# Feed-forward rows turned by VectorE in 32 by 32 blocks and moved through DRAM, in place of six TensorE transposes a tile

## The reference

```python
def _L0_attn_ref(X, W_Q, W_K, W_V):
    D = _get_D(L)                                   # 0.9 ** |n - m|
    Q = _xpos(X @ W_Q); K = _xpos(X @ W_K, downscale=True); V = X @ W_V
    p_attn = softmax(einsum('bqd,bkd->bqk', Q, K), axis=-1) * D[None, :, :]
    return einsum('bqk,bkv->bqv', p_attn, V)

def _L0_ffn_ref(x, w_gate, w_up, w_down):           # fp4_linear quantises both operands
    gate = fp4_linear(x, w_gate)                    # 256 -> 704
    y = fp4_linear(x, w_up)
    h = silu(gate) * y
    return fp4_linear(h, w_down)                    # 704 -> 256

x = x + _L0_attn_ref(_layernorm(x), W_Q, W_K, W_V)
x = x + _L0_ffn_ref(_layernorm(x), w_gate, w_up, w_down)
```

## Time and profile before

| what | value |
|---|---|
| time, three runs | 2548.14, 2549.42, 2549.66 us (median 2549.42) |
| span of the profiled execution | 2546.6 us |
| PE busy, share, instructions | 2518.4 us, 99%, 16160 |
| DVE | 2140.9 us, 84%, 4759 |
| ACT | 1489.8 us, 59%, 2966 |
| POOL | 1816.8 us, 71%, 1929 |
| DMA | 203.27 MB, 24.1% of the 16 engines on the main queue |
| HBM | 103.42 MB read, 77.59 MB written |

### The profile page before, as it was taken

One profiled execution on the slowest core, in us unless ns is written; L12 is line 12 of the kernel. 1 busy time (PEld: TensorE's weight loads), 2 busy tenths in 40 slices (PEclk: granted clock), 3 DMA queues, 4 the chain that ended last, 5 costly groups with the idle time before them and its releaser, 6 DMA issues.

```text
span 2546.6 us, 51904 instructions
## 1 busy us (share of the span) xinstructions
PE 2518.4 (99%) x16160; PEld 2290.0 (90%) x16160; DVE 2140.9 (84%) x4759; ACT 1489.8 (59%) x2966; POOL 1816.8 (71%) x1929
## 2 busy tenths in 40 slices
PE   8999999999999999999999999999999999999997
PEld 7888879999999999999999999999999999999996
DVE  8999878888878888888888888888888888888886
ACT  5766565656555655566565656565556655555654
POOL 6999956667767676667766776677666776677665
PEclk9999999999999999999999999999999999999999
DMA  8878511122111311131112111131113111211110
GB/s 285 302 271 299 186 50 30 34 86 66 38 40 45 107 37 42 34 106 42 42 34 91 62 38 40 45 107 39 42 34 106 41 42 34 95 58 38 40 38 22
DMA packets 163473, 203.27 MB, mean 80 GB/s; under 512 B 15184, under 2 KB 116752, under 8 KB 163216
## 3 DMA queue, kind: packets, MB, share of 16 engines
q1 hardware_dynamic: 163216, 200.01, 24.1%
HBM read 103.42 MB, written 77.59 MB: 71 GB/s over the span
## 4 chain that ended last, share of the span: by engine, by line
PE 85%; POOL 0%; DVE 0%; issue 0%; ACT 0%; POOLq 0%
PE score L516 27%; PE acc L655 19%; PE ring L516 19%; PE acc L516 9%; PE ring L622 6%; PE ring L675 3%; PE acc L697 1%; PE ring L613 1%; DVE hT L1226 0%; POOL probs L998 0%; ACT probs L823 0%; ACT hT L793 0%; POOL h_buf L1019 0%; POOL xv L1004 0%; POOL h_buf L1013 0%
## 5 line engine op out<-in xcount | busy, mean ns | idle before, releaser
L516 PE MATMUL score<-keys,q_st 128*128 128x512 f32 x3072 | 733.7, 394 | 3.0 <-ACT probs L823 2.6
L516 PEld LDWEIGHTS score<-keys,q_st 128*128 128x128 f32 x3072 | 567.0, 188 | 117.8 <-issue 3.0
L998 POOL TENSOR_TENSOR probs<-probs,decay 128x512 f32<-128x512 f32 (+3 forms) x416 | 450.7, 1097 | 197.5 <-ACT probs L823 197.5
L655 PE MATMUL acc<-vals,pT 128*128 128x256 f32 x3984 | 554.6, 286 | 0.8 <-DVE pT L1226 0.8
L516 PE MATMUL ring<-w_gu,xqT 128*128 128x512 f32 (+1 forms) x2304 | 509.1, 374 | 0.0
L655 PEld LDWEIGHTS acc<-vals,pT 128*128 128x128 f32 x3984 | 498.1, 189 | 7.3 <-DVE pT L1226 2.0
L516 PEld LDWEIGHTS ring<-w_gu,xqT 128*128 128x128 f32 x2304 | 419.0, 188 | 63.6 <-DVE xqT L1226 0.4
L793 ACT ACTIVATE xqT<-ring 128x256 fp32r<-128x256 f32 x128 | 49.3, 385 | 706.9 <-PE ring L613 706.9
L1239 DVE TENSOR_REDUCE smax<-score 128x1 f32<-128x1024 f32 x256 | 312.8, 1222 | 95.6 <-PE score L516 94.1
L1226 DVE TENSOR_TENSOR pT<-ring,pT 128x512 fp32r<-128x512 f32 (+3 forms) x432 | 248.7, 600 | 66.7 <-ACT pT L793 65.5
L1004 POOL TENSOR_TENSOR xv<-xv,xe 128x256 f32<-128x256 f32 x128 | 94.4, 737 | 269.1 <-DVE xv L1079 269.1
(11 more groups left out here) (133 smaller groups left out, 4470.0 us busy)
## 6 DMA issues: line engine op xcount, KB each, us to landing
k_dram<-keys SPq DMA_DIRECT2D x56, 512.0 KB, 4.5
keys<-k_dram SPq DMA_DIRECT2D x56, 512.0 KB, 7.3
edge<-vals SPq DMA_DIRECT2D x288, 64.0 KB, 2.1
q_raw<-q_dram SPq DMA_DIRECT2D x129, 128.0 KB, 2.6
x_in<-X SPq DMA_DIRECT2D x32, 512.0 KB, 4.5
q_dram<-q_stage SPq DMA_DIRECT2D x32, 512.0 KB, 5.4
x_res<-X SPq DMA_DIRECT2D x128, 128.0 KB, 2.1
out<-x_res SPq DMA_DIRECT2D x128, 128.0 KB, 1.7
```

The source lines that it names most:

```text
L516: mm = pe.matmul(dst, stat(a, k), mov(m, k), start=i == 0, stop=ends and i == n - 1)
L655: mm = pe.matmul(pv_out, pT[g % 2][:, a, j * P:(j + 1) * P], edge[places[m]][:] if kb in edges else vals[m][:, kb, :], start=i == 0, stop= ...
L998: op = pool.tensor_tensor(probs[:, k0:k1], probs[:, k0:k1], decay[:, off + k0:off + k1], ALU.mult)
```

## The change

The six transposes of PE, the two evacuations from PSUM by ACT and the two by DVE go. In their place one DVE instruction turns the 24 blocks of 32x32 in each quarter of the partitions (`h_turned_blocks`, one tile after `h_quantised`, so in step `s` for tile `s-4`), from `hq` into `h_turn`, which takes the place of the second `hq` buffer. SP writes `h_turn` to DRAM with one DMA, waits until it has landed, and reads it back with four DMAs of 32 partitions each into one of two new buffers `hqT` (`rows_turned`). In the next step ACT makes the upper part with one 128x768 instruction from SBUF (`h_transposed`), and DVE the lower part with another (`h_lower`). `down` waits for that. With only one `hq`, POOL's `h_quantised` waits until the tile before has been turned. The planned PSUM banks no longer hold `hT`; and the first tile of a batch takes its 8 blocks of probabilities in two groups of 4 in place of three (2, 3, 3), which keeps the number of banks taken in the loop divisible by three.

```diff
-XR, LAG, LATER = 8, 5, 3
+XR, LAG, TURNED = 8, 5, 4
+QUAD = 32
...
-    size = CT if 0 < t < T - 1 else CT - 1
+    size = CT if t < T - 1 else CT - 1
...
+        h_dram = nc.dram_tensor("h_dram", (2, P, CT, HK * QUAD), F32, kind="Internal").ap()
...
-        hq = [hq_buf[:, i * FT:(i + 1) * FT] for i in range(2)]
+        hq, h_turn = (hq_buf[:, i * FT:(i + 1) * FT] for i in range(2))
...
+        hqT = [sb(f"hqT{i}", [P, CT, HK * QUAD]) for i in range(2)]
...
+            def rows_turned(j, t):
+
+                g, i = j * T + t, t % 2
+                sp.wait_ge(h_turned, g + 1)
+                passed()
+                if t > 1 or not isinstance(j, int) or j:
+                    sp.wait_ge(h_split, g - 1)
+                    passed()
+                sp.dma_start(h_dram[i], h_turn.rearrange("p (c r) -> p c r", c=CT)).then_inc(turn_out, 16)
+                sp.wait_ge(turn_out, (g + 1) * 16)
+                for c in range(CT):
+                    sp.dma_start(hqT[i][c * QUAD:(c + 1) * QUAD, :, :], h_dram[i, :, c, :].rearrange("(a i) r -> i a r", a=CT)).then_inc(hqT_back[i], 16)
+
             def step(j, s, is_first, more):
...
                 if s + 2 <= T or more and not last:
                     load_q(j, s + 2, more)
+                if s >= TURNED or not is_first:
+                    rows_turned(j, s - TURNED)
...
-            def h_transposed(at, t, h):
-                if has(at, t):
-                    for ks in (range(0, CT), range(CT, HK))[h:h + 1]:
-                        if h == 0:
-                            pe.wait_ge(hq_ready, tile(at, t) + 1)
-                        dst = slot(at, "hT", t, h)
-                        for j, k in enumerate(ks):
-                            mm = pe.transpose(dst[:, j * P:(j + 1) * P], hq[t % 2][:, k * P:(k + 1) * P], ident[:])
-                        mm.then_inc(filled, 1)
...
-                    copied(at, "hT", t, 1)
+                    pe.wait_ge(h_split, tile(at, t) + 1)
...
-                    for h, n in enumerate((CT, HK - CT)):
-                        upper(hT[0][:, h * CT:h * CT + n, :].rearrange("p k t -> p (k t)"),
-                              bank(at, "hT", t, h)[:, 0:n * P], at, "hT", t, h)
+                    act.wait_ge(hqT_back[t % 2], halves(at, t) * CT * 16)
+                    if has(at, t - 1):
+                        act.wait_ge(dn_done, tile(at, t))
+                    act.activation(chunks(hT[0][:]), quads(hqT[t % 2][:]), ACT.Copy).then_inc(h_upper, 1)
...
                 attend(at, s - 1, range(min(n, 2)))
+                h_transposed(at, s - LAG)
...
+                if len(groups(s)) <= 2:
+                    meanwhile()
...
-                    if has(at, t - 2):
-                        pool.wait_ge(filled, nth(at, "hT", t - 2, 1) + 1)
+                    if has(at, t - 1):
+                        pool.wait_ge(h_turned, g)
...
+            def h_turned_blocks(at, t):
+                if has(at, t):
+                    dve.wait_ge(hq_ready, tile(at, t) + 1)
+                    if has(at, t - 1):
+                        dve.wait_ge(turn_out, tile(at, t) * 16)
+                    dve.transpose(h_turn.rearrange("p (c k j) -> p k c j", c=CT, j=QUAD), hq.rearrange("p (k c i) -> p k c i", c=CT, i=QUAD)).then_inc(h_turned, 1)
+
+            def h_lower(at, t):
+                if has(at, t):
+                    dve.wait_ge(h_upper, tile(at, t) + 1)
+                    dve.tensor_tensor(chunks(hT[1][:]), quads(hqT[t % 2][:]), chunks(hT[0][:]).bitcast(F32), ALU.subtract).then_inc(h_split, 1)
...
                 attend(at, s - 1, range(min(n, 2)))
+                h_turned_blocks(at, s - TURNED)
                 maxima(at, s, 1)
...
-                for h in range(2):
-                    h_transposed(at, s - LAG, h)
+                h_lower(at, s - LAG)
                 h_levels(at, s - 3)
```

More of the change, by code:

```diff
@@ L119, in step @@
                 take("pT", s - 1, g + 2)
-            for h in range(2):
-                if g == min(max(len(gs) - LATER, 0) + h, max(len(gs), 1) - 1) and has(s - LAG):
-                    take("hT", s - LAG, h)
         if has(s - 2):
@@ L256, in build @@
         hq_step, hv_ready, hg_ready, hq_ready = sem("hq_step"), sem("hv_ready"), sem("hg_ready"), sem("hq_ready")
+        sp_passed, h_turned, turn_out, hqT_back, h_upper, h_split = sem("sp_passed"), sem("h_turned"), sem("turn_out"), [sem(f"hqT_back{i}") for i in range(2)], sem("h_upper"), sem("h_split")
         NSTEP_W, NSTEP_LN2, NSTEP_XQ, NSTEP_HQ = 5, 2, 6, 5
@@ L286, in tile, with halves, quads, chunks @@
             return at[0] * T + t
+        def halves(at, t):
+            return at[0] * (T // 2) + t // 2 + 1
+        def quads(ap):
+            return ap.rearrange("p a (k j) -> p k a j", j=QUAD)
+        def chunks(ap):
+            return ap.rearrange("p k (a j) -> p k a j", j=QUAD)
         def nth(at, *key):
@@ L502, in _ @@
                 step(B - 1, s, False, False)
-            for t in range(T - LAG, T):
-                store(B - 1, t)
+            for s in range(T, T + LAG):
+                if s - TURNED < T:
+                    rows_turned(B - 1, s - TURNED)
+                store(B - 1, s - LAG)
             for i in range(XR):
@@ L628, in attend_begun, with attend @@
                     group(at, t, 1)
-            def attend(at, t, meanwhile, later):
+            def attend(at, t, meanwhile):
                 if not has(at, t):
                     meanwhile()
-                    later(0)
-                    later(1)
                     return
@@ L1024, in h_quantised @@
                     last, scale = (x[:, -n:].unsqueeze(1).to_broadcast([P, 2, n, QB]) for x in (blocks(hv[t % 2]), spread(hs[t % 2][:], HB)))
-                    pool.tensor_tensor(hq[t % 2][:, F - HALF:FT].rearrange("p (a b k) -> p a b k", a=2, k=QB), last, scale, ALU.mult)
-                    pool.tensor_tensor(blocks(hq[t % 2][:, 0:F - HALF]), blocks(hv[t % 2][:, 0:F - HALF]), spread(hs[t % 2][:, 0:HB - n], HB - n), ALU.mult).then_inc(hq_ready, 1)
+                    pool.tensor_tensor(hq[:, F - HALF:FT].rearrange("p (a b k) -> p a b k", a=2, k=QB), last, scale, ALU.mult)
+                    pool.tensor_tensor(blocks(hq[:, 0:F - HALF]), blocks(hv[t % 2][:, 0:F - HALF]), spread(hs[t % 2][:, 0:HB - n], HB - n), ALU.mult).then_inc(hq_ready, 1)
             def step(at, s):
@@ L1252, in attend @@
                     lower(pT[g % 2][:, 1, 0:n], bank(at, "pT", t, g)[:, 0:n], pT[g % 2][:, 0, 0:n], at, "pT", t, g)
-            def h_transposed(at, t, h):
+            def h_turned_blocks(at, t):
                 if has(at, t):
-                    for n in (CT, HK - CT)[h:h + 1]:
-                        hi, lo = (hT[i][:, h * CT:h * CT + n, :].rearrange("p k t -> p (k t)") for i in range(2))
-                        lower(lo, bank(at, "hT", t, h)[:, 0:n * P], hi, at, "hT", t, h)
+                    dve.wait_ge(hq_ready, tile(at, t) + 1)
[6 more added lines that the diff above has]
+                    dve.tensor_tensor(chunks(hT[1][:]), quads(hqT[t % 2][:]), chunks(hT[0][:]).bitcast(F32), ALU.subtract).then_inc(h_split, 1)
             def residual(at, t):
```

8 lines of the change are left out of this document (3 added, 5 removed).

## The result

The changed kernel takes 2781.99 us (median of 4 runs, 2777.37 to 2786.25) against 2549.54 for the kernel before on the same chip: a ratio of 1.091, 95% interval 1.0894 to 1.0925. Forecast were 2745 and a range of 2630 to 2915. So it is slower, as said, and by 232 us in place of 196.

A forecast was written before the change was run, and what follows sets the result against it. PE was taken to set the pace before the change. Profiled 2546.6 + 177 (14.8 and 8 us a batch, 7.75 batches) + 10 tail + 10 batch ends = 2743.6; with 2.8 to the median 2746, rounded to 2745; range 2630 to 2915.

The forecast's parts named there:

- The ring: `xv`, POOL to `hq`, turning, DVE from second maximum to `xv`: no slack, 18.27 us in the step shown, plus 14.8 a batch.
- The turning: DVE's new transpose instruction ahead of the second maximum: 0.98 us, not held by POOL; rival: held or slow, 2912, chance 0.14.
- The holding: DVE's `h_levels` instructions run against POOL's decays and last longer: between -0.7 and +2.4 us a step, +0.5 taken.
- The second term: POOL and DVE meeting in `h_levels` and the decays: +0.5 us a step, 8 us a batch.
- PE's transposes: Six removed a tile, 67 us if PE stayed the bound; claimed to buy nothing. Rival PE stays the bound: 2482, chance 0.05.
- The trip: Turned row through DRAM and back: 10 to 13 us, fitting in 18; rival longer than a step: 3117, chance 0.07.
- The 20 us for tail and batch ends: 10 us for the open DRAM trip in the tail, 10 for late edges at 7 batch ends, 1.5 each.
- The sum: Step length round the ring: 5.03 + 0.98 + 12.38 - 1.10 + 0.98 = 18.27 us, without DVE's 2.16 of waits for ACT.
- the rival of the clock: PE idles 1 to 2 us a step and its clock falls: 2.0 us a step, 2993, chance 0.05.
- the falsifiers: Signs of being wrong: PE at 99%, the turning far from 1 us, or DVE's first idle time at the DMA.

The follow-up runs named there:

- before_wait: The kernel before the change, plus only a DVE wait for `hq` of tile s-4 ahead of the second maximum: 2694.18 us, ratio 1.0564.
- ring_held: The changed kernel, with POOL beginning the decays of tile s only after DVE has ended `h_levels` of tile s-3: 2764.38 us, ratio 1.0842.
- pe_refilled: The changed kernel, with PE making six transposes of the identity a tile that nothing reads: 2780.78 us, ratio 1.0904.
- trip_twice: The changed kernel, with the turned row written to DRAM a second time, after the first write landed, into a buffer nobody reads: 2793.21 us, ratio 1.0944.
- before_turn: The kernel before the change, plus DVE waiting for `hq` of tile s-4 and turning it into a spare buffer nobody reads: 2800.73 us, ratio 1.0979.
- turn_later: The changed kernel, with the turning moved from ahead of the second maximum to behind the last group of probabilities: 2676.97 us, ratio 1.0493.

## Why the prediction was right, and what it missed

*The ring.* Right, in place and size. Predicted were a wait of DVE ahead of the turning in nearly every step, 250 us in all: 127 times, 241.0. Predicted a step of 18 to 19 us: 302.9 / 16 = 18.9. That the ring closes without the change's own work is shown by `before_wait`.

*The turning.* 0.98 taken, 978 ns measured. It did not wait for POOL: in the step above it runs while POOL's L1035 is under way (1417.95 to 1419.34), and takes the same 0.98. The rule of the Trainium skill, page "SBUF — State Buffer", section "Who interferes with whom", that one SBUF input outside the two-port modes does not contend, would have it so; the trace agrees. The estimate of 1.87 us from the Trainium skill's page "VectorE: DVE Perf Modes", section "The three transpose paths", is not borne out. The subtraction took 950 ns for 0.98.

*The holding.* The second term was +0.5 us a step. The groups give, mean after less mean before in ns: L1101 on `h_buf` +484, L1097 +94, L1094 -44, L1324 +111, L1338 -137, together +0.51. What `ring_held` adds is that most of it could not be taken back by holding POOL.

*PE's transposes.* Worth nothing, as said: `pe_refilled` shows it.

*The trip.* Here two errors met and did no harm, which is luck. The trip was given 10 to 13 us and takes 5.9 on median from the first issue to the last landing (in the step above 2.35 to the first issue back, then four issues in 1.74, each landed 2.1 after it starts). The time it has was given as 18 us and is less: from the end of the turning to the start of ACT's copy are 14.2 us in this step (1419.10 to 1433.26), 11.2 on median and 9.5 at the least before the tail. A trip of 10 to 13 us would have lain open in many steps. As it is, the row lands 2.4 to 8 us before ACT starts on it in all but the last step of a batch. That a trip 2.3 us longer is still hidden is shown by `trip_twice`. The 20 us for tail and batch ends came to 17.

*What was mis-sized: the ring without its idle time.* The batch came to 302.9 where 275.6 + 22.8 = 298.4 was forecast, 4.5 a batch or 35 us. (Less 3 for the tail that makes 32 in the span; the rest of the 37 between 2745 and 2782 is mostly that the profiled execution is the fastest of the four.) By parts, the mean of 96 steps of six batches against the forecast, in us (the forecast of the last part is what 298.4 / 16 leaves for it):

| part of the ring | forecast | measured |
|---|---|---|
| end of `xv` to end of POOL's `hq` | 5.03 | 5.03 |
| from there to the start of the turning | 0 | 0.15 |
| start of the turning to the second maximum | 0.98 | 0.90 |
| from there to the end of the next `xv` | 12.64 | 12.85 |
| together | 18.65 | 18.93 |

The sum started the turning at the instant at which `hq` ends (in the step above 1416.70 + 1.28 = 1417.98, and the turning starts at 1418.12). In `before_turn`, where the turning has one wait ahead of it and not two, only 0.03 us lie there; that this is the reason is not shown. And the sum took all of DVE's waits for ACT out of the step ("which go when DVE is the late one"). They did not all go: those for ACT's `pT` and `hT` did (0.2 and 1.6 us left in all), but in these 96 steps 0.23 us a step of waiting for `h_buf` stayed.

Part of that is the clock, and the step above shows how. Busy time by stretch, with the granted clock behind the engines:

```profile
1412.95:1421.40 8.45, 5.70 (x38) 4.95 (x36) 5.54 (x11) 2.49 (x4) 6.70 (x7) 1.00 0.28 95
1421.40:1425.90 4.50, 4.46 (x24) 4.47 (x25) 4.19 (x6) 2.96 (x6) 3.04 (x3) 0.62 0.41 117
1425.90:1432.95 7.05, 7.05 (x47) 6.52 (x46) 5.59 (x19) 4.03 (x9) 2.83 (x4) 1.00 0.00 1
```

PE sat idle for 2.79 us, and then the granted clock is 0.62, between the lower level of 1.2 GHz and the upper of 2.4. The 24 products take 4.63 us, where 12 took 1.66 at the full clock earlier in the step. Gate and up, silu and so `h_buf` come late by that, and DVE waits 0.99 us for them in this step, in three pieces.

What it costs can be read where the same place of a batch runs once at the full clock and once not: here the step that ends with `xv` of a batch's fifteenth tile, from `xv` to `xv`, in two batches, and PE in it.

```profile
882.67:900.21 17.54, 14.88 (x94) 13.40 (x93) 14.04 (x33) 7.84 (x14) 11.13 (x13) 1.00 0.76 271
1183.54:1202.15 18.61, 15.90 (x92) 14.15 (x91) 14.08 (x34) 8.84 (x17) 11.11 (x13) 0.91 0.75 262
```

```profile
891.14 1.69 PE L687 MATMUL acc<-vals,pT 128*128 128x256 f32 x12 [2.65 <-DVE pT L1248]
892.67 3.97 PE L550 MATMUL ring<-w_gu,xqT 128*128 128x512 f32 x18
...
1192.02 2.04 PE L687 MATMUL acc<-vals,pT 128*128 128x256 f32 x12 [2.71 <-DVE pT L1248]
1193.86 5.20 PE L550 MATMUL ring<-w_gu,xqT 128*128 128x512 f32 x18
```

With nearly the same idle time of PE before it, the second ran partly at the lower level, gate and up took 1.23 us more, DVE waited 1.29 us for ACT's `h_buf` where it had stood idle for 0.41, and the step is 1.07 us longer. Of the 108 steps from the second batch to the last four tiles, 24 had the lower level in them. Those 24 have 22.0 of the 27.7 us that DVE waited for `h_buf`. For 17 of them the same place ran in another batch at the full clock: they are 10.8 us longer together, but behind three of them the next step is 1 us shorter, so some 8 us are left. The other seven stand at one place that never ran at the full clock; at 1.07 us each they would add 7. So the rival of the clock, given 0.05 and 2 us a step, is there in small, with some 8 to 15 us, less than half of the 35. No run with the turning in the ring is at the full clock: `pe_refilled` has 0.979, `before_turn` 0.982.

Of the falsifiers none came: PE is at 91%, the turning at 1 us, and DVE's longest wait is for POOL.

## What to carry to other kernels

A wait costs by what it closes, not by what it waits for. Before putting one into a tuned loop, follow it round: if the producer itself waits, in the same step, for something the consumer's engine does a little earlier, the two make a ring, and everything on it counts in full or nearly so, however much slack either engine's busy share shows. Then move the wait behind work that is free of it, and look in the profile what the freed time makes meet: here 140 of 241 us came back as longer instructions, which no wait view lists and only the mean durations show.

## What was not expected of the hardware

- The time inside a DVE instruction that POOL holds is large when the two run in phase: in `turn_later` a `tensor_scalar` over 704 columns took 1.13 us on average, where it takes 0.53 unheld and 0.62 in the changed kernel, and DVE's busy share went from 83 to 91%, with the same instructions.
- A wait of POOL for DVE (the decays held) made the kernel 3.7% faster (2676.97 to 2578.3).
- Idle time of PE of 2.6 to 2.8 us was followed by a stretch partly at the lower level in some steps (2.71 us at 1192.02) and not in others (2.65 us at 891.14), in a kernel whose mean granted clock stays at 0.977; in the kernel before, the clock is full from 400 us up to the tail.
- The instruction behind `STREAM_TRANSPOSE` on DVE starts 0.90 us after it, although it is listed with 0.98, and between the end of POOL's instruction and the start of DVE's that waits for it lie 0.15 us on average, 0.03 in `before_turn`.
